# A two-layer attention and ternary feed-forward kernel: order of VectorE and ScalarE work in its second layer

## The reference

```python
qkv = x @ W_qkv.T;  Q = qkv[..., :D]
coef = (alpha * beta_q + (1.0 - alpha) * beta_k) * scale * tau
scores = coef * einsum('bsd,bnd->bsn', Q, K_mem)          # K_mem = V_mem = the context, 256 rows
scores = scores - max(scores)
thr = top_k(scores, 54)[0][..., -1:]                       # keep the 54 largest of 256
att = softmax(where(scores < thr, -inf, scores))
x = x + einsum('bsn,bnd->bsd', att, V_mem) @ W_o.T
...
def bit_linear(x, w):                                      # both operands quantised
    s = 127 / clip(max(abs(x)), EPS);  qx = clip(round(x * s), -128, 127) / s
    g = 1.0 / clip(mean(abs(w)), EPS); qw = clip(round(w * g), -1, 1) / g     # ternary weights
    return qx @ qw.T
h = silu(bit_linear(x, w_gate)) * bit_linear(x, w_up)      # 512 -> 2048
x = x + bit_linear(rms_norm(h, ln_weight), w_down)         # 2048 -> 512
```

## Time and profile before

| | |
|---|---|
| time, three runs | 1634.51 us median (1630.48 to 1636.3) |
| profiled execution | 1627.65 us, of which the span is 1626.4 us |
| TensorE clock granted, mean | 0.981 |
| busy: PE, DVE, ACT, POOL | 1512.7, 1155.5, 976.5, 690.6 us |
| chain that ended last | PE 68%, DVE 18%, ACT 6%, issue 5% |

### The profile page before, as it was taken

One profiled execution on the slowest core, in us unless ns is written; L12 is line 12 of the kernel. 1 busy time (PEld: TensorE's weight loads), 2 busy tenths in 40 slices (PEclk: granted clock), 3 DMA queues, 4 the chain that ended last, 5 costly groups with the idle time before them and its releaser, 6 DMA issues.

```text
span 1626.4 us, 26610 instructions
## 1 busy us (share of the span) xinstructions
PE 1512.7 (93%) x8842; PEld 1183.9 (73%) x8842; DVE 1155.5 (71%) x2977; ACT 976.5 (60%) x2488; POOL 690.6 (42%) x832
## 2 busy tenths in 40 slices
PE   5899999999999999999988899999996799999987
PEld 4778888888888888888876566666665566666653
DVE  4777777677777767777777655555567888888774
ACT  3666666566656666666656665666654366666655
POOL 2445455464645555545565200000014445555443
PEclk8999999999999999999999999999999799999999
DMA  6011111111110111111335666666664101111000
GB/s 266 14 39 67 40 62 43 40 66 40 53 53 39 66 48 48 62 40 52 118 134 219 231 244 217 222 216 213 227 218 164 27 8 53 53 47 40 27 14 27
DMA packets 50824, 156.71 MB, mean 96 GB/s; under 512 B 5888, under 2 KB 6016, under 8 KB 49280
## 3 DMA queue, kind: packets, MB, share of 16 engines
q1 hardware_dynamic: 50688, 155.02, 27.0%
HBM read 113.05 MB, written 41.94 MB: 95 GB/s over the span
## 4 chain that ended last, share of the span: by engine, by line
PE 68%; DVE 18%; ACT 6%; issue 5%; DMA 2%; POOL 1%; SPq 0%; DVEq 0%; ACTq 0%; POOLq 0%
PE bank L289 10%; PE bank L1145 10%; PE bank L319 9%; PE bank L372 9%; PE quad L359 5%; PE quad L1174 3%; PE bank L1199 3%; PE quad L347 2%; PE quad L349 2%; PE quad L348 2%; DVE bh L2052 2%; DVE wk L2008 2%; PE bank L1615 2%; PE bank L331 2%; PE quad L1707 2%
## 5 line engine op out<-in xcount | busy, mean ns | idle before, releaser
L537 ACT ACTIVATE Pt<-Pt,small 128x384 f32<-128x384 f32 (+1 forms) x256 | 172.8, 682 | 118.4 <-DVE small L756 118.2
L319 PE MATMUL bank<-wq,xT 128*128 128x512 f32 x768 | 207.0, 405 | 3.9 <-DVE wq L651 3.3
L372 PE MATMUL bank<-PT,vv 128*128 128x512 f32 x672 | 200.2, 406 | 10.0 <-DVE PT L741 6.2
L963 POOL TENSOR_SCALAR Pt<-Pt,small 128x384 f32<-128x384 f32 (+1 forms) x256 | 162.5, 647 | 86.6 <-DVE small L764 86.5
L756 DVE CUSTOM_DVE_ANT_0 Pt<-quad,mask,small 128x384 f32<-128x384 f32 (+1 forms) x256 | 171.3, 679 | 27.5 <-PE quad L349 26.2
L1145 PE MATMUL bank<-wq,ot 128*128 128x512 f32 x768 | 189.5, 399 | 0.9 <-DVE xr L1323 0.9
L741 DVE TENSOR_TENSOR PT<-quad,PT 128x512 fp32r<-128x512 f32 x224 | 154.1, 688 | 42.0 <-ACT PT L529 41.2
L1145 PEld LDWEIGHTS bank<-wq,ot 128*128 128x128 f32 x768 | 142.8, 189 | 33.1 <-issue 1.5
L319 PEld LDWEIGHTS bank<-wq,xT 128*128 128x128 f32 x768 | 137.9, 190 | 30.5 <-DVE wq L651 4.6
L951 POOL TENSOR_TENSOR t<-t 128x512 f32<-128x512 f32 x64 | 84.0, 1312 | 151.3 <-DVE t L722 151.3
L372 PEld LDWEIGHTS bank<-PT,vv 128*128 128x128 f32 x672 | 116.7, 190 | 33.4 <-DVE PT L741 14.5
(11 more groups left out here) (274 smaller groups left out, 3544.5 us busy)
## 6 DMA issues: line engine op xcount, KB each, us to landing
ot_scratch<-OT SPq DMA_DIRECT2D x64, 512.0 KB, 2.7
ot<-ot_scratch SPq DMA_DIRECT2D x64, 512.0 KB, 3.5
wkv_f<-in_w SPq DMA_DIRECT2D x12, 512.0 KB, 5.8
wkc_f<-in_w SPq DMA_DIRECT2D x12, 512.0 KB, 6.5
wkv_f<-in_wg SPq DMA_DIRECT2D x11, 512.0 KB, 4.3
wkv_f<-in_wd SPq DMA_DIRECT2D x11, 512.0 KB, 5.0
wkv_f<-in_wu SPq DMA_DIRECT2D x10, 512.0 KB, 5.3
stg<-in_ctxT SPq DMA_DIRECT2D x16, 256.0 KB, 3.3
```

The lines of the kernel that those rows point to most:

```text
L319: ins = pe.matmul(bQ[:], xT[p][:, k, qt * 128:qt * 128 + 128], wq[j][:, g, k, :], start=(part == 0 and k == 0), stop=(part == 2 and k == 3))
L372: ins = pe.matmul(bO[:], vv[x][:, bg % 2, kt, :], PT[y][:, k % 2, :], start=(kt == 0 and n == 0), stop=(kt == tiles_in(i) - 1 and n == 2))
L537: act.activation(p, p, ACT.Exp, bias=nm[:, i % 2, h:h + 1], scale=-1.0, accum_out=sm[:, i % 2, h:h + 1]).then_inc(f["s_exp"], 1)
L963: pool.tensor_scalar(p, p, ri[:, i % 2, h:h + 1], 1.0, ALU.mult, ALU.mult).then_inc(f["p_n"], 1)
```

## The change

Four edits, all in the order of work or in which engine does it:

1. Stages 2 to 8: the two masked-probability instructions (`dve_pm`) go from behind `dve_h` of quarter 3 to in front of it, directly behind the last round. The first `dve_hmax` goes from in front of that `dve_h` to behind it.
2. Stages 2 to 8: `dve_fc` is split. The sum of squares (`dve_f_var`, two small instructions) stays, then comes the low part of the attention output's first half, then the rest of `dve_fc`, then the second half.
3. Chunks 42 to 47: ScalarE rounds them and VectorE clips, and the loads behind them wait for ScalarE's pass (`t_lev`).
4. `ffn0`'s end and stages 0 and 1: the last tile's squares go in front of the query cast on ScalarE; the first two rounds of sequence 0 go into stage 0, between and ahead of its `dve_xT`; the second half of stage 1's query product is cut in two, and the turn of the probabilities stands between.

```diff
@@ def sp_w(ks):
-            elif k - 3 in both:
+            else:
                 sp.wait_ge(f["t_lev"], 2 * (mem["shared"] + done[k - 3]))
-            else:
-                sp.wait_ge(f["w_ter"], 16 + done[k - 3])
@@ ffn0: def act_program():
+            for j in range(2):
+                act_square(n, j)
             if n == NT - 1:
                 l1["act_qT"](0, 0)
-            for j in range(2):
-                act_square(n, j)
...
         l1["act_ctx"](0, 0)
+        act_l(42)
+        act_l(43)
@@ def dve_l(k):
-        v.did(dve.tensor_scalar(out3, r, gm[:, 2:3], None, ALU.is_lt))
-        v.settle()
-        dve.scalar_tensor_tensor(out3, r, gm[:, 1:2], out3, ALU.is_gt, ALU.subtract).then_inc(f["w_ter"], 1)
+        mem["dve_clip"](chunk(k), mem["shared"] + both.index(k))
@@ layer1: def pe_program():
             if s == 1:
                 pe_xb(s, 0)
-                pe_xb(s, 1)
+                pe_xb(s, 1, (0,))
             if o_:
                 pe_xd(o)
+            if s == 1:
+                pe_xb(s, 1, (1,))
@@ layer1: def act_program():
             if s == 1:
                 act_qT(s, 0)
-                act_qT(s, 1)
             if o_:
                 act_pT(o)
-            if x_ and s != 1:
+            if x_:
                 act_qT(s, 1)
...
+            if s == 1:
+                ffn["act_l"](47)
...
             if s == 0:
                 act_ctx(s, 1)
+                for k in (44, 45, 46):
+                    ffn["act_l"](k)
@@ def dve_gate_up(n, rounds, q=None, m=None, b_pm=None):
         for j in range(4):
+            if j == 3 and b_pm is not None:
+                dve_pm(b_pm)
             dve_h(n, j)
...
-            if j == 2:
+            if j == (2 if b_pm is None else 3):
                 dve_hmax(n, 0)
@@ layer1: def dve_program():
-            left = [(o, r) for r in range(6)] if o_ else []
-            if s > 1:
-                left = left[3:]
+            left = [(o, r) for r in range(2 if s == 1 else 3, 6)] if o_ else []
...
             if f_:
-                dve_fc(n)
+                dve_f_var(n)
             dve_last(s, 0)
             if o_:
                 dve_oT(o, 0)
+            if f_:
+                dve_fc(n)
+            if o_:
                 dve_oT(o, 1)
...
             if x_:
                 dve_top(2 * s)
                 dve_top(2 * s + 1)
+            if s == 0:
+                dve_round(s, 0)
             if s + 1 < NB:
                 dve_xT(2 * s + 2)
+            if s == 0:
+                dve_round(s, 1)
```

More of the change, by code:

```diff
@@ L1053, in visits @@
         return [k for k in range(ends[n], ends[n + 1]) if seq[k][0] == kind]
-    both = [k for k in range(ends[NT - 2]) if seq[k][0] == "T"]
+    both = [k for k in range(48) if seq[k][0] == "T"]
     def chunk(k):
@@ L1358, in dve_l @@
     def dve_l(k):
-        gm, out3, r = gam1[:, seq[k][1], :], chunk(k), wraw[k % 3]
-        dve.wait_ge(f[f"g_w{k % 3}"], 16 * (k // 3 + 1))
-        v.did(dve.tensor_scalar(out3, r, gm[:, 2:3], None, ALU.is_lt))
-        v.settle()
-        dve.scalar_tensor_tensor(out3, r, gm[:, 1:2], out3, ALU.is_gt, ALU.subtract).then_inc(f["w_ter"], 1)
+        mem["dve_clip"](chunk(k), mem["shared"] + both.index(k))
     def dve_up(n):
@@ L1404, in dve_program @@
     def dve_program():
-        last = visits(NT - 2, "T")
         dve.wait_ge(f["w_sum"], 2)
@@ L1429, in dve_program @@
                 l1["dve_qT"](0, 0)
-                dve_l(last[0])
             if n == 0:
@@ L1436, in dve_program @@
                 for k in visits(n, "T"):
-                    mem["dve_clip"](chunk(k), mem["shared"] + both.index(k))
-        dve_l(last[1])
+                    dve_l(k)
+        dve_l(42)
+        dve_l(43)
     def pool_rs(n):
@@ L1457, in ffn0 @@
     return {"programs": (pe_program, act_program, dve_program, pool_program, sp_program), "pe_y": pe_y,
-            "sp_ot": sp_ot, "sp_x": sp_x, "sp_w2": sp_w2, "sp_w": sp_w, "dve_l": dve_l,
-            "last": visits(NT - 2, "T")[2:] + visits(NT - 1, "T")}
+            "sp_ot": sp_ot, "sp_x": sp_x, "sp_w2": sp_w2, "sp_w": sp_w, "act_l": act_l, "dve_l": dve_l}
 def layer1(nc, a, f, mem, x2_dram, out, ffn):
@@ L1597, in pe_xa_turn, with pe_xb @@
         ins.then_inc(f["xat_mm"], 1)
-    def pe_xb(b, j):
+    def pe_xb(b, j, parts=(0, 1)):
         if j == 0:
@@ L1609, in pe_xb @@
             pe.wait_ge(f["x3"], 2 * b - 3 + j)
-        for mm in range(2):
+        for mm in parts:
             m0 = (2 * j + mm) * 128
@@ L1617, in pe_xb @@
                     n += 1
-        ins.then_inc(f["aq_mm"], 1)
+        if 1 in parts:
+            ins.then_inc(f["aq_mm"], 1)
     def pe_xc(n):
@@ L2058, in dve_hmax, with dve_f_var @@
                                 ALU.max, apply_absolute_value=True))
-    def dve_fc(n):
+    def dve_f_var(n):
         c = col(n)
@@ L2065, in dve_fc @@
         dve.tensor_scalar(c[:, 49:50], c[:, 48:49], 1.0 / 2048, 1e-6, ALU.mult, ALU.add).then_inc(f["h_var"], 1)
+    def dve_fc(n):
+        c = col(n)
         dve_hmax(n, 1)
@@ L2081, in dve_x4, with dve_gate_up @@
         dve.scalar_tensor_tensor(x, bM[:], col(n)[:, 55:56], x, ALU.mult, ALU.add).then_inc(f["x4"], 1)
-    def dve_gate_up(n, rounds, q=None, m=None):
+    def dve_gate_up(n, rounds, q=None, m=None, b_pm=None):
         for j in range(4):
+            if j == 3 and b_pm is not None:
+                dve_pm(b_pm)
             dve_h(n, j)
@@ L2095, in dve_gate_up @@
                 dve_qT(q, 0)
-            if j == 2:
+            if j == (2 if b_pm is None else 3):
                 dve_hmax(n, 0)
     def dve_last(s, part):
-        first, end = {(0, 0): (0, 1), (1, 0): (1, 2), (1, 1): (2, 4)}.get((s, part), (0, 0))
-        for k in ffn["last"][first:end]:
+        first, end = {(1, 0): (44, 46), (1, 1): (46, 48)}.get((s, part), (0, 0))
+        for k in range(first, end):
             ffn["dve_l"](k)
@@ L2108, in dve_program @@
             o, n = s - 1, 2 * (s - 2)
-            left = [(o, r) for r in range(6)] if o_ else []
-            if s > 1:
-                left = left[3:]
+            left = [(o, r) for r in range(2 if s == 1 else 3, 6)] if o_ else []
             if f_:
-                dve_gate_up(n, left, s if x_ else None)
-                left = left[4:]
-            for b, r in left:
-                dve_round(b, r)
-            if o_:
+                dve_gate_up(n, left, s if x_ else None, None, o if o_ else None)
+            elif o_:
+                for b, r in left:
+                    dve_round(b, r)
                 dve_pm(o)
@@ L2122, in dve_program @@
                 dve_qT(s, 0)
-                dve_qT(s, 1)
             if o_:
@@ L2162, in dve_program @@
             if f_:
+                dve_f_var(n + 1)
                 dve_fc(n + 1)
```

## The result

The changed kernel takes 1607.38 us (median of 4 runs, 1603.95 to 1609.92) against 1632.49 for the kernel before beside it (4 runs, 1628.77 to 1636.3): ratio 0.9847, interval 0.983 to 0.9864. The forecast was 1614.4, its range 1607 to 1623. The profiled execution took 1606.86 us (span 1605.5), 20.8 less than before's; the sum of the prediction was 20.1.

The account below looks back on a forecast made before the run. TensorE, busy 93%, was taken to bound the kernel, its idle time mostly waits for the masked-probability pair. 6.6 + 5.4 + 6.8 + 1.3 = 20.1 us off the median 1634.5 gave 1614.4 us, range 1607 to 1623.

Parts of the forecast that it names:

- Edit 1, steady stages: Stages 3 to 7: TensorE's wait of 1.08 us ahead of `pe_xd` goes, both `pm` instructions take 0.48.
- Edit 2: Steady stages: the 0.68 us wait ahead of `pe_xc` goes, a new wait of 0.40 comes for the second `aoT`.
- Stage 2: The pair's wait falls from 4.28 to 1.5 us and the clock stays at its upper level; 5.4 us gained.
- Stage 1: Stages 0 and 1, edits 3 and 4: earlier squares, moved rounds and no two-pass chunks gain 6.6 us.
- stands still for 2.65 us: Stage 1, ahead of `pe_xd`: TensorE waits 2.65 us, not 4.25, with the clock perhaps staying up.
- Rival 1: Stage 1: the clock falls in the 2.65 us ahead of `pe_xd`, costing 2.4 us: 1616.8; chance 0.30.
- Stage 8: The wait of 1.76 us goes, the second `aoT` gives 0.49 back; 1.3 us gained.
- granted clock 1.00 from 1290 on: Sign that the prediction is right: TensorE's clock at its full level from 1290 us on.
- Rival 2: Stages 3 to 7: the second `aoT` takes the wait's place, losing their gain: 13.3 us, 1621.2; chance 0.06.
- Rival 4: Stage 1: ScalarE, in order, waits for loads of visits 45 and 46; 1640.5 at 26 us lateness; chance 0.03.
- Rival 5: TensorE isn't waiting for the pair but for other inputs right behind it; 3.5 us gained, 1631.0; chance 0.05.
- Rival 3: Stage 1: clips 44 to 47 held behind GpSimd instructions, 5.1 us on VectorE; 1619.5 at worst; chance 0.06.

Follow-up runs that it names:

- e_pm: Kernel before with edit 1 alone: the masked-probability pair directly behind the last search round in stages 2 to 8; 1616.4 us, ratio 0.9926.
- e_norounds: Changed kernel with rounds 0 and 1 of sequence 0 back in stage 1; 1611.58 us, ratio 0.9893.
- e_last2: Changed kernel with both low parts of the attention output ahead of the rest of the scale in stages 7 and 8 alone; 1607.53 us, ratio 0.9843.
- e_fc: Kernel before with edit 2 alone: `dve_fc` split, first low part of the attention output ahead of the rest of the scale; 1630.52 us, ratio 1.0003.
- e_pmbh: Kernel before with the masked-probability pair behind the fourth hidden quarter but ahead of the reduction; 1620.16 us in one execution.
- e_whole: Changed kernel with stage 1's second query half in one piece again, ahead of the turn of the pair; 1608.45 us, ratio 0.9858.
- e_inter: Changed kernel with each of the two rounds of sequence 0 behind its `dve_xT` in place of ahead; 1609.85 us, ratio 0.9863.
- e_late: e_inter with ScalarE's cast of sequence 1's context moved behind its cast of the probabilities; 1607.62 us, ratio 0.9847.
- e_3: Kernel before with edit 3 alone: chunks 42 to 47 rounded by ScalarE and clipped by VectorE; 1629.25 us, ratio 0.9984.

## Why the prediction was right, and where its steps were not

**Edit 1, steady stages.** Right: no wait in stages 3 to 8, both instructions at 0.48. The size was 1.33 a stage, not 1.08: without the wait the stretch that held it (last output product to `pe_xd`) is 1.25 shorter in e_pm, and the turn behind it takes 0.60 for 0.66. The other 0.17: where TensorE need not wait, `pe_xd` starts 0.17 us before the down product's last row ends (1329.73 against 1328.87 + 1.03 in the changed kernel). A wait costs that overlap too.

**Edit 2.** Right: 0.43 for 0.40, net 0.26 for 0.28. The stage fell by 1.57 (predicted 1.36), to 42.44.

**Stage 2.** Nearly right: columns c and d gave 7.2, predicted 2.8 + 2.4 + 0.28 and the 1.08 of stage 3, 6.6. The clock stayed up, as predicted, but the wait is 2.36, not 1.5: before, TensorE was at 0.50 until 1284 and later at the turn for it; now it is back at 1.00 after 1276 and there sooner. The length of this wait says little: in kernels with the same stage 2 it is 1.50 (e_norounds) to 3.32 (e_last2), and column c stays at 20.3 to 20.9.

**Stage 1.** The total was near (a + b gave 7.0, predicted 6.6), and so were the steps, up to the clock. They have to be read from a common point. Against stage 0's score product (1238.24 before, 1238.08 after) the last `axT` starts 1.62 us later than in the earlier trace rows, since round 0 stands ahead of the *first* `axT` and delays the bank that the second turn needs; the squares take back 1.41. That leaves 0.21, and the prediction had 0.2.

```profile
1243.86 0.69 DVE L1971 TENSOR_TENSOR axT<-bank,axT 128x512 fp32r<-128x512 f32 x1
...
1246.05 0.69 DVE L1971 TENSOR_TENSOR axT<-bank,axT 128x512 fp32r<-128x512 f32 x1
```

`pe_xd` starts 15.83 us behind the score product, predicted 15.91 (1252.75 less 1238.24 - 1.4), and `pe_xe` 18.18, predicted 18.36. What was wrong is the sentence that TensorE "stands still for 2.65 us" ahead of `pe_xd` with the clock up. It doesn't stand still there at all: the clock fell around the waits for `axT`, the 36 matmuls took 7.03 us for 4.57, and these 2.46 us used up the slack of 2.65. The prediction looked at the clock in one wait only and not in the wait of 3.04 that its own delay of `axT` makes. Rival 1 had the right price and the wrong place. That the fall cost nothing is luck, by 0.2 us; where the clock falls in this stage goes with what it did in column a. In the kernel before and e_fc the 48 matmuls run in 6.01 and 6.02 us and the clock is lost in the pair's wait; with the same instructions e_pm and e_pmbh take 8.64 and 8.52, come out 1.3 better in column b and had lost 1.3 to 1.6 in column a.

**Stage 8.** Predicted 1.3, measured nothing in the profiled execution: column f gave 2.01, 0.28 of it stage 7's edit 2 (as in e_fc), and g took 1.75 back. The wait of 1.76 went. But "0.49 back" was read from the earlier trace rows, where the two `aoT` stand 2.24 us apart because ScalarE's second cast came from a product at the lower clock (4.62 us). At full clock they stand 1.42 apart (e_pm: 1555.31 and 1556.73), and 0.61 + 2.12 between them then costs 1.3. That term of the sum was mis-sized: with the clock up in both, column g is 12.3 without edit 2 (e_pm) and 13.9 with it (e_whole), 1.5 us. The rest is the clock. Behind the wait of 2.45 it fell in the changed kernel, e_norounds, e_inter and e_late, and the output product took 7.34 for 5.78; behind the same wait in e_whole it did not:

```profile
1550.32 5.78 PE L1669 MATMUL bank<-ao,aoT 128*128 128x512 f32 x24 [2.45 <-DVE aoT L1986]
```

e_last2, with the shorter wait of 1.16, has 12.6. The sign "granted clock 1.00 from 1290 on" therefore failed: in the changed kernel the clock is at 0.50 from 1549.4 to 1552.8 and again from 1597.2 to 1600.6, ahead of the last down product.

**The rest.** The squares' 1.4 is right (column a: 1.41, with the clock at 1.00 in both profiles). Rival 2 didn't come (no steady stage lost). Rival 4 neither: ScalarE's passes over visits 44 to 46 start without a wait. Rival 5 falls with the waits: where the pair was early, no other releaser took its place. Rival 3 came in small. Of the four late clips, two at 1257.91 took 0.75 us together, two at 1262.08 0.90, beside a GpSimd instruction of one column. What paid at 1258 was GpSimd, whose scaling of `axn` began beside the clips and took 1.10 where its twin took 0.78:

```profile
1258.13 1.10 POOL L2206 TENSOR_SCALAR axn<-xs_a,bcl 128x512 f32<-128x512 f32 x1
...
1263.11 0.78 POOL L2206 TENSOR_SCALAR axn<-xs_a,bcl 128x512 f32<-128x512 f32 x1
```

Beside the second pass of a chunk, before, it had taken 1.45 (1260.43 there), so the clips cost GpSimd less than what they replace. The larger price is that of two-input instructions: VectorE's wait for GpSimd's to end in stage 3 before, in e_pmbh, in e_3 and in e_inter, up to 1.0 us each. The Trainium skill's page SBUF — State Buffer, section "SBUF: two separate sides", gives the shared port to whichever starts first, for the whole instruction; the traces agree in both directions (1.48 against 0.48 on VectorE, 1.10 against 0.78 on GpSimd).

The median gained 25.1 us where the profiled pair differs by 20.8; the interval allows 22 to 28. The forecast of 1614.4 is 7.0 high. 2.0 of these lie in its starting value: the median before was 1634.51 with three runs and 1632.49 with the fourth. 1.9 are the stretches (22.0 for 20.1). The other 3.1 are what the medians gained beyond the 22.0 of one execution each; no run explains them.

## What to carry to other kernels

Put what releases the engine that bounds ahead of everything that only fills the list, and look at what the neighbour on GpSimd does in that slot: the same instruction took 0.48 or 1.48 us by one place in the order. Where a filler goes ahead of a short instruction that another engine waits for, work out that engine's slack: here the two rounds made TensorE's chain 1.6 us later, it had 2.65, and putting both rounds behind gained nothing (e_late: column b 29.38 for 28.58). A duration on which a margin rests must be read at the clock that the changed kernel will have there. Two traces are compared from an instruction that both have, not by absolute times. In the last stages, where no next input comes in, the stretches show another best order than in the steady ones; the whole times don't show it yet.

## What the runs showed of the hardware

The instructions alone don't fix where the clock falls. In four profiles with the same stage 1 it came about the waits of 1.49 and 1.40 us in two (e_pm, e_pmbh, and in both once more behind the pair's wait) and only in the wait of 4.25 in the other two (before, e_fc). The two kinds differ already in column a, where the clock had fallen in e_pm and e_pmbh and not in the others; e_3 and e_norounds go with the first kind, e_inter and e_late with the second. Behind a wait of 2.45 us in stage 8 it fell in four profiles and not in a fifth (e_whole).

Whether a fall costs depends on whether the work that it hits is waited for: nothing of the 2.46 us in the changed kernel's 36 matmuls, all of the 1.56 in stage 8's output product (column g 15.40 for e_whole's 13.85).

The second instruction of the pair (two inputs of 128x256 in SBUF), begun while GpSimd worked on tensors in SBUF, ended 0.3 us behind GpSimd's instruction: 1.47 to 1.49 us in place of 0.48, in stage 3 before, in e_pmbh, e_3 and e_inter.
